# Embedding products of a ViT tower regrouped into three pairs per chunk, each pair with its own wait

## The reference, cut to what matters

```python
p = x.reshape(b, c, nph, PH, npw, PW)
p = p.transpose(0, 2, 4, 1, 3, 5).reshape(b, nph * npw, c * PH * PW)   # 16 x 36 x 768
h = jnp.einsum('bnd,ed->bne', p, Wp) + bp                             # 16 x 36 x 192
...
h = _layernorm(h + _L0_attn_ref(h, ...))
h = _layernorm(h + _L0_ffn_ref(h, ...))
```

## Time and profile before

| | before |
|---|---|
| median of three runs | 118.58 us |
| the three runs | 113.70, 118.58, 118.98 us |
| the profiled execution's own time | 113.86 us |
| its span (first to last instruction) | 111.7 us |
| TensorE matmul busy | 100.1 us, 90%, 1349 matmuls |
| VectorE busy | 78.5 us, 70% |
| ScalarE busy | 71.1 us, 64% |
| GpSimd busy | 30.1 us, 27% |
| read from HBM | 7.08 MB |

### The profile page before, as it was taken

One profiled execution on the slowest core, in us unless ns is written; L12 is line 12 of the kernel. 1 busy time (PEld: TensorE's weight loads), 2 busy tenths in 40 slices (PEclk: granted clock), 3 DMA queues, 4 the chain that ended last, 5 costly groups with the idle time before them and its releaser, 6 DMA issues.

```text
span 111.7 us, 3468 instructions
## 1 busy us (share of the span) xinstructions
PE 100.1 (90%) x1349; PEld 89.8 (80%) x1349; DVE 78.5 (70%) x239; ACT 71.1 (64%) x198; POOL 30.1 (27%) x42
## 2 busy tenths in 40 slices
PE   6989999999999999999999999999959868797940
PEld 4778998998998889789988998998948767684910
DVE  0566909955991887319686888988867779988670
ACT  4678687577659965976865558662366366558260
POOL 4003626699914500000591630000005400000000
PEclk9999999999999999999999999999999999999997
DMA  3999999300000000000000000000000000000202
GB/s 75 355 336 387 414 421 426 126 0 0 6 3 6 3 6 0 0 6 0 0 0 6 0 6 0 0 6 0 3 0 6 3 0 0 6 0 0 65 20 79
DMA packets 4123, 7.73 MB, mean 69 GB/s; under 512 B 1292, under 2 KB 2444, under 8 KB 3980
## 3 DMA queue, kind: packets, MB, share of 16 engines
q1 hardware_dynamic: 3740, 7.24, 17.8%
q10 hardware_dynamic: 368, 0.28, 0.8%
HBM read 7.08 MB, written 0.44 MB: 67 GB/s over the span
## 4 chain that ended last, share of the span: by engine, by line
PE 61%; DVE 16%; ACT 7%; DMA 5%; issue 5%; SPq 3%; DVEq 0%; ACTq 0%
PE proj L920 11%; PE outp L1050 8%; PE score L1005 7%; DMA x_f<-x_t 5%; PE proj L905 4%; PE trans L1029 3%; PE outp L884 3%; PE proj L909 3%; PE proj L906 3%; PE proj L912 3%; PE proj L913 3%; PE proj L1067 2%; ACT ln_ln L562 2%; DVE ln_st L733 2%; PE proj L1072 1%
## 5 line engine op out<-in xcount | busy, mean ns | idle before, releaser
L548 ACT ACTIVATE pt_t<-trans,image_t 108x216 f32<-108x216 f32 (+1 forms) x42 | 14.5, 420 | 1.4 <-PE trans L1029 1.3
L424 POOL TENSOR_TENSOR h_res<-h_hi,bias 128x288 f32<-128x288 f32 x8 | 5.2, 666 | 23.3 <-DVE h_lo L757 23.2
L532 ACT ACTIVATE score<-d_t 128x296 f32<-128x296 f32 (+2 forms) x16 | 6.5, 409 | 6.2 <-DVE d_t L697 6.1
L1005 PE MATMUL score<-k_t,q_t 64*36 64x37 f32 (+1 forms) x416 | 10.3, 196 | 0.0
L1005 PEld LDWEIGHTS score<-k_t,q_t 64*36 64x36 f32 x416 | 9.0, 111 | 1.2 <-issue 0.6
L707 DVE TENSOR_REDUCE sm_t<-score 128x8 f32<-128x288 f32 (+1 forms) x16 | 6.9, 434 | 2.8 <-ACT score L532 2.8
L726 DVE TENSOR_TENSOR x_lo<-outp,x_hi 128x288 fp32r<-128x288 f32 x12 | 5.4, 452 | 4.9 <-ACT x_hi L555 4.8
L694 DVE TENSOR_REDUCE mx_t<-score 128x8 f32<-128x296 f32 (+2 forms) x16 | 7.1, 444 | 2.4 <-PE score L1013 1.4
L920 PE MATMUL proj<-wv_hi,h_hi 128*108 128x384 f32 (+1 forms) x24 | 8.3, 344 | 0.2 <-DVE wv_hi L659 0.2
L562 ACT ACTIVATE ln_ln<-ln_mv,const 108x1 f32<-108x1 f32 (+1 forms) x12 | 3.5, 293 | 7.3 <-DVE ln_mv L736 7.3
L651 DVE TENSOR_TENSOR x_lo<-x_f,x_hi 128x288 fp32r<-128x288 f32 x12 | 6.8, 580 | 1.8 <-ACT x_hi L464 1.8
(11 more groups left out here) (192 smaller groups left out, 335.7 us busy)
## 6 DMA issues: line engine op xcount, KB each, us to landing
ffn_f<-f_w SPq DMA_DIRECT2D x1, 1088.0 KB, 12.1
wqk_f<-w_qk SPq DMA_DIRECT2D x2, 512.0 KB, 7.9
x_f<-x_t SPq DMA_DIRECT2D x2, 432.0 KB, 6.3
wv_f<-w_v SPq DMA_DIRECT2D x1, 768.0 KB, 7.1
wo_f<-w_out SPq DMA_DIRECT2D x1, 768.0 KB, 9.5
x_f<-x_t SPq DMA_DIRECT2D x2, 288.0 KB, 4.8
tw_f<-tok_w SPq DMA_DIRECT2D x2, 256.0 KB, 4.3
wqk_f<-w_qk SPq DMA_DIRECT2D x2, 256.0 KB, 5.6
```

Of the source, the lines that this page charges most:

```text
L548: nc.scalar.activation(pt_t[:, n % 2, 0:tiles, :, i], trans[0:ROWS, 0:tiles, :, 0:TOK], ACT.Copy, scale=image_t[:, i:i + 1]).then_inc(spli ...
L1005: ins = nc.tensor.matmul(s[64 * h:64 * h + TOK, im, 0:width], q, k_t[rows, n % QK_RING, im, 0:width], start=(kind == "attn" and im == 0), ...
```

## The change

`embed` issues the same six matmuls per chunk on the same operands into the same two banks, in another order. Before, all three products of half 0 stood ahead of those of half 1, behind one wait for the low parts. Now there are three pairs, each pair over both halves: (`tw_hi`, `x_hi`), then (`tw_lo`, `x_hi`), then (`tw_hi`, `x_lo`). The first pair waits for the high parts, the second for `tok_lo`, the third for `x_lo_s`. Group 0 has four waits per chunk in place of two, group 1 two in place of one. The order of the steps on TensorE and all that the other engines do is the same.

```diff
             def embed(n):
                 g, k = divmod(n, PK)
+
+                def chunk(w, x, first, last):
+                    for m in range(NCH):
+                        cols = slice(128 * m, 128 * m + 128)
+                        ins = nc.tensor.matmul(embed_bank[g][m][:, 0:GT], w[:, k, cols], x[:, g, k],
+                                               start=(k == 0 and first), stop=(k == PK - 1 and last))
+                        if k == PK - 1 and last:
+                            ins.then_inc(embedded, 1)
+
+                if g == 0:
+                    pe.wait_ge(tok_hi, n + 1)
+                pe.wait_ge(x_hi_s, n + 1)
+                chunk(tw_hi, x_hi, True, False)
                 if g == 0:
                     pe.wait_ge(tok_lo, n + 1)
+                chunk(tw_lo, x_hi, False, False)
                 pe.wait_ge(x_lo_s, n + 1)
-                for m in range(NCH):
-                    cols = slice(128 * m, 128 * m + 128)
-                    for z, (a, b) in enumerate(((tw_hi, x_hi), (tw_hi, x_lo), (tw_lo, x_hi))):
-                        ins = nc.tensor.matmul(embed_bank[g][m][:, 0:GT], a[:, k, cols], b[:, g, k],
-                                               start=(k == 0 and z == 0), stop=(k == PK - 1 and z == 2))
-                    if k == PK - 1:
-                        ins.then_inc(embedded, 1)
+                chunk(tw_hi, x_lo, False, True)
```

## The result

| | before | changed |
|---|---|---|
| median of 14 runs each | 113.91 us | 113.39 us |
| lowest | 113.63 us | 113.13 us |
| profiled execution | 113.86 us | 113.31 us |
| its span | 111.7 us | 111.1 us |
| value projection starts in its trace | 19.15 us | 18.55 us |

The ratio is 0.9955, with a 95% interval of 0.9940 to 0.9971: 0.5 us saved, within 2%. Two more measurements of the same change gave 0.9989 (0.9964 to 1.0014) and 0.9965 (0.9935 to 0.9995); they are among the experiments. Of the kernel before there were three runs ahead of the prediction and eleven more behind it, and its median went from 118.58 to 113.91: the two runs near 119 were of a rarer kind.

What follows compares the result with a forecast made beforehand. TensorE's matmul queue was taken as the bound, its beginning held by the transfer and low parts. Chunk 6's 0.48 plus chunk 7's 0.12 less 0.2 for `h_lo` gave 0.40 us; 118.58 became 118.2 us, range 113.0 to 119.2.

Steps and rivals of the forecast that it cites:

- the last of the sum: Whole kernel: the 0.40 us saving subtracted from the median of three runs, 118.58, giving 118.2 us.
- faster by far: Embedding: fewer holes make a late-rising clock rise early, removing the 4.7 us between runs; median 113.4 us, chance 0.09.
- Nothing gained: Chain behind `qk 0`: something that does not move, nearest the landing of `wv_f`, ends the gain; 118.5 us, chance 0.13.
- A queue of matmuls without holes: TensorE from 20 us on: matmuls without gaps, busy 49.55 of 50 us to 70 us, so its end moves with its beginning.
- the walk through the stage: Embedding to `qk 0`: chunk 2 gains 0.49 us, lost at chunk 6; chunk 6 gains 0.48, chunk 7 0.12 more, `h_lo` returns 0.2.
- so this chunk no longer restarts: Chunk 7: four matmuls cover its `x_lo` by 0.05 us, the price of a wake-up; gain at `qk 0` 0.60 us.
- The prediction's sign of being wrong: Embedding: a wait for `x_lo` ahead of a chunk's fifth matmul would say VectorE is later than four matmuls.
- That `h_lo` takes back 0.2 us: `qk 0`: the first matmul on `h_lo` waits for it and restarts, giving back 0.2 us of the gain.
- the added waits and the bank changes: Embedding: waits already met and consecutive matmuls going to two banks in turn were each taken to cost 0.
- the rival "slower": Chunks 0 to 7: the new order keeps TensorE at the lower clock, 3.7 us later, 122.3 us; chance 0.04.
- the race behind the value weights: Value weights: VectorE's last step comes ahead of GpSimd's subtraction, done 0.55 us earlier, 0.21 counting; 118.0 us, inside the range.

Runs made afterwards that it cites:

- the two halves of the change: Changed kernel with the split waits only in chunks 0 to 5, or only in chunks 6 to 11; ratios to the kernel before 1.0004 and 0.9971.
- group 1 alone: Changed kernel with the split waits only in chunks 6 to 11, chunks 0 to 5 waiting for both low parts first; ratio to the kernel before 0.9971.
- The order alone: Changed kernel with the three pairs in the new order but both low-part waits ahead of the chunk as before; ratio to the kernel before 0.9997.
- the longer warm-up: 32 warm-up matmuls in place of 20, in the changed kernel and in the kernel before; ratios to the kernel before 1.0044 and 1.0028.

## Why the prediction was right or wrong

**Wrong: the level.** The step that failed is the last of the sum, "so I move the saving to the median as it is: 118.58 - 0.40 = 118.2". The saving was about right (0.5 us measured, then 0.1 and 0.4) and the time was 4.8 us off. A median of three values, two of them 5 us above the third and above the profiled execution, was taken for where the kernel lies. Over all its runs beside these kernels the kernel before was above 117 us in 14 of 119, so two among three was a rare draw, about one in 26. The stated range, 113.0 to 119.2, held both levels and so holds the measured time; that says nothing for the forecast inside it. The number 113.5, which the text worked out from the profiled execution, was the forecast to give: 113.39 was measured. The sentence that "no row of the trace shows what those 4.7 us are" was true, and should have led to the execution that could be read.

The rival "faster by far" named 113.4, which is the number measured, and that is luck. It rested on the same two runs, put their cause into the embedding and expected the change to remove them. But most runs of the kernel before take 113.9, and the changed kernel was above 117 us in 7 of 38 runs (3, 0 and 4 in its three measurements), which is no fewer. The third trace of the change is of such an execution, and it shows another place. Windows of the changed kernel in that execution (start:end, length, busy of PE, PEld, DVE, ACT, POOL, granted clock, DMA share, GB/s):

```profile
90.00:95.00 5.00, 3.58 (x56) 3.04 (x56) 4.10 (x20) 3.27 (x9) 0.00 (x0) 0.86 0.00 0
95.00:100.00 5.00, 4.77 (x50) 3.95 (x47) 3.29 (x10) 1.81 (x7) 0.00 (x0) 0.50 0.02 3
100.00:105.00 5.00, 4.92 (x38) 4.55 (x37) 3.53 (x14) 2.49 (x10) 0.00 (x0) 0.61 0.00 0
```

The granted clock is 0.50 through 95 to 100 us, the lower level, behind a stretch in which TensorE was busy 3.58 of 5 us; the embedding of this execution is at full speed. From the value projection to the end it takes 115.3 - 18.79 = 96.5 us in place of 92.55: the missing 4 us. The trace of the changed kernel with 14 warm-up matmuls, of a run of 118.66 us, is the same: 0.50 from 95 to 100, and 97.4 us behind the value projection. The runs near 119 of the kernel before have no trace, so that theirs is the same cause is argued from these two.

The stretch of 3.58 us does not bring the fall about by itself. The kernel before has it too, at full clock, and in the first trace of the change the clock falls earlier, which costs nothing: 92.55 us behind the value projection all the same. First the kernel before, then the changed kernel:

```profile
90.00:95.00 5.00, 3.58 (x65) 3.07 (x63) 4.28 (x22) 3.27 (x9) 0.00 (x0) 1.00 0.00 0
```

```profile
90.00:95.00 5.00, 4.87 (x76) 4.39 (x77) 4.31 (x21) 3.72 (x10) 0.00 (x0) 0.85 0.01 3
```

What decides when it falls stays open.

**Right: what bounds it and what it hangs on.** The value projection's start carries over one to one: 92.55 us behind it before and after. "Nothing gained" fell with this. "A queue of matmuls without holes" from 20 us on said too much: the rows it rests on end at 70 us, and from 90 to 95 TensorE is busy 3.58 of 5 us. That what lies behind 70 us moves along all the same is shown by the 92.5 to 92.7 us, not by those rows.

**Right in the main: the walk through the stage**, where the transfer lands as in the trace it was made from. Prediction and third trace: chunk 2 at 7.20 and 7.11, right behind chunk 1, since its `x_hi` was ready at 6.95; chunk 6 at 10.86 and 10.85, released by `x_hi`; `qk 0` at 12.57 and 12.63; the first matmul on `h_lo` at 13.47 and 13.48, with its restart of 0.23 behind it; the value projection at 18.75 and 18.79. The 0.49 won at chunk 2 and lost at chunk 6 is what the two halves of the change show, 0.0 and 0.3 us. The sum was 0.40; the three ratios are 0.5, 0.1 and 0.4 us.

One step of the walk failed there: "so this chunk no longer restarts". The fifth matmul of chunk 7 was due 0.1 us behind its `x_lo` (12.30 and 12.20), and in the third trace it comes at 12.27 with the same `x_lo`, yet from that pair to `qk 0` are 0.36 us in place of 0.26. It restarts, and chunk 7 brings 0.06 us more than chunk 6, not 0.12. The time doesn't show it, since `h_lo`, ready at 13.42, holds `qk 0` behind that anyway.

**Incomplete: one execution's starts as constants.** The sum took the landing of the third transfer (10.33) and TensorE's arrival at chunk 0 (5.37) as given. Neither is. ScalarE's first `x_hi` of group 1 starts between 9.98 and 10.75 in the fourteen traces of before, after and the experiments, and with the same 20 warm-up matmuls chunk 0 starts between 5.01 and 6.01 (6.39 in the execution of 185 us below). Nor is 0.46 us for the `x_lo` of chunk 6: it took 1.04 in the second trace of the change and 0.77 in that of group 1 alone. The prediction's sign of being wrong, a wait inside a chunk for `x_lo`, is there in the latter.

What the old order would have done in the other two executions of the change can be estimated from their rows, with 0.05 us from a low part to the start and 0.11 for a restart. In the first trace `x_lo` of chunk 6 is ready at 10.94 and TensorE comes at 10.97; that of chunk 7 is ready at 11.86 and TensorE comes at 11.76. Only chunk 7 would have waited, and `qk 0` would start near 12.8 in place of 12.56: the change has some 0.3 of the 0.6 us, the rest is that this execution's transfer landed earlier. In the second trace chunk 6 would have waited until 11.55, and `qk 0` would start near 13.25 in place of 12.77: some 0.5 us. By this estimate the change pays in all three, 0.3 to 0.5 us, and the 0.1 us of the second measurement stays unexplained; its interval allows for 0.4. That `h_lo` takes back 0.2 us holds in the third trace and not in the other two: in the first it is ready at 13.08 and the matmul on it follows at 13.35 without a pause.

**Right: the added waits and the bank changes cost nothing.** The order alone measured 0.9997, its matmuls 0.13 us apart; it has the bank changes and not the added waits. Those are in the change, whose chunks 3 to 5, with four waits each that are met, run their pairs 0.25 to 0.28 us apart in all three traces. The rule that the rival "slower" took from the Trainium skill, TensorE: Matmul & The Clock Gate, section "A second HAM failure mode: psum-queue depth-cycling", did not show: chunks 0 to 7 change the bank at each of 48 matmuls and run at 0.13 us, the level of 2.4 GHz, from the step of the clock on, in every trace of the new order but the one of 185 us, wherever they don't wait.

**Not shown: the race behind the value weights.** VectorE's last step took 1.52 us in the change too, with GpSimd's subtraction 0.03 ahead of it (16.96 and 16.99); the order did not turn in the other traces either, with GpSimd 0.02 to 0.04 ahead.

## What to carry to other kernels

A wait for several operands ahead of a group of matmuls was split here at no cost that shows, the products that need least going first. It pays by the lateness of the last operand, as far as the matmuls put ahead cover it, and only in the groups behind which no later transfer holds the engine again. The gain is gone when the engine arrives late, as with the longer warm-up. Work the gain out for two arrivals of the engine and two landings of the transfer, not for one trace's, and make sure which of the two sets the next group. And where a few run times fall on two levels, forecast at the level of the execution that was profiled, since its sum is the only one that can be made, and say which level is meant.

## What the runs showed of the hardware

The clock of TensorE has a part in the kernel's beginning that I had not counted on. The warm-up matmuls take 0.21 us each where all 20 run alike (1.05 to 5.29), the level of 1.2 GHz, with the granted clock at 1.00 in that stretch too, and the step to 2.4 GHz comes at a time that differs from execution to execution of the same code: the two 384-column matmuls behind them start 0.32 us before the next one in some executions (5.02 to 5.34) and 0.64 in others (5.29 to 5.93).

Once it did not come at all. In the profiled execution of the kernel with the split waits in group 0 alone, TensorE ran at half speed from end to end, 185.3 us, while the granted clock read 1.00 in every window; TensorE in order of time and a window of it:

```profile
7.01 0.64 PE L882 MATMUL score<-x_hi,tw_lo 128*128 128x288 f32 x2
7.49 0.74 PE L882 MATMUL score<-x_lo,tw_hi 128*128 128x288 f32 x2
```

```profile
10.00:50.00 40.00, 40.00 (x219) 35.44 (x219) 13.74 (x28) 15.13 (x34) 15.49 (x22) 1.00 0.27 108
```

The pairs are 0.48 to 0.58 us apart in place of 0.26 to 0.27, while ScalarE and VectorE take as long for their steps as ever (1.11 us for the `x_hi` of chunks 6 to 8, 0.94 for `h_lo`). The granted clock therefore doesn't show this kind of slowness; the distance between equal matmuls does. What starts it stays open, and with one such execution nothing says whether the edit has a part in it. Two runs of 159 us, one of the kernel before and one of the change, had a mean granted clock of 0.57 and 0.56, so there the same column did show it, and so did it in a run of 125.67 us of the kernel before with 14 warm-up matmuls, with 0.75.
